# Maxima passes of a causal attention stage as one stream over its blocks, block 1's in the stage before, and both borders of the stage woven

## The reference

```python
# C: attention
q = x @ Wq + bq; k = x @ Wk + bk; v = x @ Wv + bv
scores = jnp.einsum('bqd,bkd->bqk', q, k) / jnp.sqrt(jnp.float32(hd))
scores = jnp.where(causal, scores, -jnp.inf)
weights = jax.nn.softmax(scores, axis=-1)
out = jnp.einsum('bqk,bkd->bqd', weights, v) @ Wo + bo
# D: routed feed-forward
base_out = jnp.einsum('bsd,df->bsf', x, W_base) + b_base
shared_out = jnp.einsum('bsr,rf->bsf', jnp.einsum('bsd,dr->bsr', x, A_s), B_s)
gates = jax.nn.softmax(jnp.einsum('bsd,de->bse', x, W_router) + b_router, axis=-1)
topk_w, topk_i = jax.lax.top_k(gates, TOP_K)          # TOP_K = 2 of E = 6
...
routed_out = jnp.einsum('bser,erf->bsf', hw, B_r)     # hw: h times its expert's weight
return base_out + shared_out + routed_out
# around each layer: x = _layernorm(x + layer(x))
```

## Time and profile before

| what | us |
|---|---|
| median of 3 runs | 1553.93 (1552.56 to 1555.5) |
| the profiled execution's own time | 1553.85 |
| its span in the profile | 1552.1 |
| TensorE busy in the span | 1471.6 (95%) |
| VectorE busy | 1006.4 (65%) |
| ScalarE busy | 735.5 (47%) |
| GpSimd busy | 342.1 (22%) |
| mean granted clock of TensorE | 0.986 |

### The profile page before, as it was taken

One profiled execution on the slowest core, in us unless ns is written; L12 is line 12 of the kernel. 1 busy time (PEld: TensorE's weight loads), 2 busy tenths in 40 slices (PEclk: granted clock), 3 DMA queues, 4 the chain that ended last, 5 costly groups with the idle time before them and its releaser, 6 DMA issues.

```text
span 1552.1 us, 23859 instructions
## 1 busy us (share of the span) xinstructions
PE 1471.6 (95%) x9484; PEld 1008.5 (65%) x9484; DVE 1006.4 (65%) x1967; ACT 735.5 (47%) x1040; POOL 342.1 (22%) x259
## 2 busy tenths in 40 slices
PE   8999999999999977898999999989989998989998
PEld 6677777777777765444554555546656655567886
DVE  3355545464635455897778878775878877556665
ACT  4433333333333322878877876854334344442333
POOL 0021112121111122000000000001657676750001
PEclk9999999999999989999999999999999999999999
DMA  7203131303031150001101100014000000000112
GB/s 264 79 27 108 33 102 54 105 29 106 35 100 48 40 189 21 28 1 55 54 13 43 55 28 28 1 41 115 33 0 1 1 0 1 0 1 28 55 55 82
DMA packets 43904, 79.93 MB, mean 51 GB/s; under 512 B 7073, under 2 KB 14881, under 8 KB 42386
## 3 DMA queue, kind: packets, MB, share of 16 engines
q1 hardware_dynamic: 43794, 78.41, 15.0%
HBM read 53.24 MB, written 25.17 MB: 51 GB/s over the span
## 4 chain that ended last, share of the span: by engine, by line
PE 60%; issue 20%; DVE 14%; ACT 4%; POOL 2%; DMA 0%; SPq 0%; DVEq 0%; POOLq 0%; ACTq 0%
PE psum L125 12%; PE psum L127 11%; PE psum L126 11%; PE psum L1335 5%; PE psum L978 3%; PE psum L985 3%; DVE sm L447 3%; PE psum L594 2%; PE psum L620 2%; PE psum L1313 2%; PE psum L615 2%; PE psum L609 2%; DVE c_mx L1256 1%; PE psum L624 1%; PE psum L629 1%
## 5 line engine op out<-in xcount | busy, mean ns | idle before, releaser
L978 PE MATMUL psum<-early,high 128*128 128x512 fp8e4 x1024 | 234.5, 381 | 10.3 <-DVE low_r L950 4.2
L978 PEld LDWEIGHTS psum<-early,high 128*128 128x128 fp8e4 x1024 | 98.1, 98 | 132.1 <-ACT early L857 6.7
L1184 POOL TENSOR_TENSOR c_ls<-c_ls,c_pr 128x512 f32<-128x512 f32 (+2 forms) x136 | 161.6, 1188 | 66.1 <-ACT c_pr L1229 56.9
L393 POOL TENSOR_TENSOR rms<-ms,mhalf 128x16 f32<-128x16 f32 x32 | 93.1, 2911 | 364.4 <-DVE ms L456 364.4
L1229 ACT ACTIVATE c_pr<-c_sc 128x512 f32<-128x512 f32 (+2 forms) x144 | 85.4, 594 | 159.8 <-DVE c_sc L1271 145.4
L1335 PE MATMUL psum<-c_pr,V 128*128 128x512 f32 (+2 forms) x288 | 139.0, 568 | 5.2 <-ACT c_pr L1229 3.9
L125 PE MATMUL psum<-Qh,Kh 128*128 128x512 f32 (+1 forms) x272 | 141.9, 522 | 0.0
L1271 DVE TENSOR_TENSOR c_sc<-psum,c_mb 128x512 f32<-128x512 f32 (+2 forms) x144 | 92.1, 641 | 50.4 <-PE psum L127 37.4
L985 PE MATMUL psum<-high,b_act 128*128 128x512 fp8e4 x512 | 116.7, 382 | 0.3 <-ACT early L861 0.3
L125 PE MATMUL psum<-early_r,high_r 128*128 128x512 f32 x256 | 106.5, 416 | 5.4 <-DVE early_r L419 5.4
L127 PE MATMUL psum<-Qh,Kl 128*128 128x512 f32 (+1 forms) x272 | 104.8, 385 | 0.0
(11 more groups left out here) (230 smaller groups left out, 3248.8 us busy)
## 6 DMA issues: line engine op xcount, KB each, us to landing
low<-x_dram SPq DMA_DIRECT2D x9, 1024.0 KB, 5.6
wst<-in_L_ffn_w_gating SPq DMA_DIRECT2D x16, 512.0 KB, 4.5
xs<-in_L_attn_x SPq DMA_DIRECT2D x8, 1024.0 KB, 7.5
xt<-in_x_turned SPq DMA_DIRECT2D x7, 1024.0 KB, 4.9
x_dram<-xs SPq DMA_DIRECT2D x7, 1024.0 KB, 4.9
x_dram<-low SPq DMA_DIRECT2D x5, 1024.0 KB, 4.3
wst<-in_L_ffn_w_linear SPq DMA_DIRECT2D x16, 256.0 KB, 4.6
high<-x_dram SPq DMA_DIRECT2D x4, 1024.0 KB, 6.8
```

The costliest lines, as they stand in the source:

```text
L393: nc.gpsimd.tensor_tensor(rms[:, :], ms[:, :], const["mhalf"][:, 0:H], ALU.pow).then_inc(*done)
L978: last = t.matmul(out[:, h, :], w8g[:, tile + k, (2 * m + h) * P:(2 * m + h + 1) * P], x8[:, u, k, :], start=k == 0, stop=k == DC - 1)
L1184: nc.gpsimd.tensor_tensor(ls[:, i % 2, q0:], ls[:, i % 2, q0:], pr[:, g % SLOTS, q0:], ALU.add).then_inc(*L.done(*name))
```

## The change

**One stream.** The maxima of blocks 2 to 7, 132 jobs, are one list, taken along by all tiles of blocks 0 to 6 (112 tiles). Each block's maxima are due two tiles before its `mb`, and at each tile as many are taken as the tightest due time asks for, rounded up. This gives two at each of the first 22 tiles (blocks 0, 1 and ten tiles of block 2) and one at each tile after that. The number of maxima jobs in blocks 0 to 6 goes from 8, 12, 16, 20, 24, 28, 32 to 8, 16, 22, 16, 20, 24, 26.

**Block 1's maxima** leave block 0 for the end of stage B. The plan puts (1, 0, 0) and (1, 0, 1) after block 0's and the other six behind the bias row and the projections of block 7, two in a row at each place. A pair shares a bank (`w = 4 + name[2] % 2`), so its second matmul waits until VectorE has read the first. Block 0's own maxima move behind `y` (7, 0) and `y` (7, 1) of stage B.

**The weights of D**: ScalarE's high part is now made two tiles before VectorE's low part, which stays where it was.

**The opening of D**: `x` (0, 0) to (0, 3), `h` (0), `hN` (0), the gates of block 0 in six pieces and `hT` (0) are put between the last eighteen tiles of block 7. After the last `pv` come `x` (1), `rb` (0, 0), `L` (7), `rr` (0, 0), `h` (1), `y` (7, 0), `y` (7, 1), `hN` (1), `rb` and `rr` (0, 1), `y` (7, 2), `y` (7, 3) and the rest. The four `y` (7, c) use banks 7, 0, 1, 2 in place of 3, 7, 6, 7. The weighted result `hw` moves to a part of `Qh`, since `Ql` is still read then.

The core of the diff:

```diff
-    order = max_jobs(0) + [("mb", 0), ("bias", 0)]
+    order = max_jobs(0) + max_jobs(1)[:2] + [("mb", 0), ("bias", 0)] + max_jobs(1)[2:]
+    ahead = [job for i in range(2, NB) for job in max_jobs(i)]
+    due, n = [], -2
+    for i in range(1, NB - 1):
+        n += tiles(i)
+        due.append((n + tiles(0), sum(len(max_jobs(j)) for j in range(2, i + 2))))
...
-        ahead = max_jobs(i + 1) if i + 1 < NB else []
...
-            take = -(-len(ahead) // max(1, n - 2 - k)) if ahead else 0
+            gone = n_ahead - len(ahead)
+            take = max([-(-(jobs - gone) // (end - g)) for end, jobs in due if end > g and jobs > gone], default=0)
...
-        elif i == 0 and kind in ("mx", "mb"):
-            w = 4 + (name[2] % 2 if kind == "mx" else 0)
+        elif i == 0 and kind == "mb":
+            w = 4
+        elif i <= 1 and kind == "mx":
+            w = 4 + name[2] % 2
...
         elif kind == "y" and i == NB - 1:
-            w = (3, 7, 6, 7)[name[2]]
+            w = (7, 0, 1, 2)[name[2]]
...
-    order = [("x", 0, k) for k in range(DC)] + [("h", 0)] + [("x", 1, k) for k in range(DC)]
-    order += [("hN", 0), ("rb", 0, 0), ("rb", 0, 1), ("rb", 0, 2), ("hT", 0), ("h", 1), ("rr", 0, 0), ("hN", 1),
-              ("rr", 0, 1), ("rr", 0, 2), ("rb", 0, 3), ("rr", 0, 3), ("hT", 1)]
+    order = [("x", 0, k) for k in range(DC)] + [("h", 0), ("hN", 0)] + [("gate", 0, n) for n in range(6)] + [("hT", 0)]
+    order += [("x", 1, k) for k in range(DC)] + [("rb", 0, 0), ("rr", 0, 0), ("h", 1), ("hN", 1), ("rb", 0, 1), ("rr", 0, 1)]
+    order += [("rb", 0, 2), ("rr", 0, 2), ("hT", 1), ("rb", 0, 3), ("rr", 0, 3)]
...
+        plan += part("B", ("y", last, 3), ("VT", last - 1)) + part("C", ("mb", 0), ("mx", 1, 1, 1))
+        plan += part("B", ("VT", last - 1), ("V", last - 1)) + part("C", ("mx", 1, 1, 1), ("mx", 1, 2, 1))
+        plan += part("B", ("V", last - 1), ("Q", last)) + part("C", ("mx", 1, 2, 1), ("mx", 1, 3, 1))
+        plan += part("B", ("Q", last), ("VT", last)) + part("C", ("mx", 1, 3, 1), ("s", 0, 1)) + part("B", ("VT", last), None)
...
-        splits = {("s", 3, 2): 0, **{("s", 6, 3 * k + 2): k + 1 for k in range(DC + 1)}}
...
+        opening = {("pv", last, 14 + n): job for n, job in [(k, ("x", 0, k)) for k in range(DC)] + [(5, ("h", 0)), (7, ("hN", 0)), (15, ("hT", 0))]}
+        opening.update({("pv", last, 22 + n): ("gate", 0, n) for n in range(6)})
+        high_parts = {("s", 3, 0): 0, **{("s", 6, 3 * k): k + 1 for k in range(DC + 1)}}
+        low_parts = {("s", i, k + 2): n for (_, i, k), n in high_parts.items()}
```

More of the change, by code:

```diff
@@ L1078, in stage_c @@
         order += tail
+    assert not ahead
     order += [("L", NB - 1)] + [("y", NB - 1, c) for c in range(CH)]
@@ L1412, in stage_d @@
     gate = [(x, None) if isinstance(x, str) else x for x in gate]
-    dve_order, act_order, pool_order, counts = [], [], [], []
-    for n, name in enumerate(order):
+    gate_pieces = [gate[:3], gate[3:6], gate[6:10], gate[10:14], gate[14:19], gate[19:]]
+    pe_order, dve_order, act_order, pool_order, counts = [], [], [], [], []
+    for name in order:
         kind, b = name[0], name[1]
+        if kind != "gate":
+            pe_order.append(name)
         if kind == "x":
@@ L1424, in stage_d @@
         elif kind == "hN":
-            act_order.append(("exp", b))
-            dve_order += [(g, b, c) for g, c in gate]
+            if b:
+                act_order.append(("exp", b))
+                dve_order += [(g, b, c) for g, c in gate]
+        elif kind == "gate":
+            if name[2] == 0:
+                act_order.append(("exp", b))
+            dve_order += [(g, b, c) for g, c in gate_pieces[name[2]]]
         elif kind == "hT":
@@ new lines, in program @@
+        high_parts = {("s", 3, 0): 0, **{("s", 6, 3 * k): k + 1 for k in range(DC + 1)}}
+        low_parts = {("s", i, k + 2): n for (_, i, k), n in high_parts.items()}
+        for job in part("C", ("s", 0, 1), ("y", last - 1, CH - 1)) + part("C", ("y", last - 1, CH - 1), ("pv", last, NB * CH - 1)):
+            plan.append(job)
+            if job[1] in high_parts:
+                plan.append(("D", ("ahead", "act", high_parts[job[1]])))
+            if job[1] in low_parts:
+                plan.append(("D", ("ahead", "dve", low_parts[job[1]])))
+            if job[1] in opening:
+                plan.append(("D", opening[job[1]]))
```

38 lines of the change are left out of this document (21 added, 17 removed).

## The result

The changed kernel takes 1542.02 us (median of 4 runs, 1540.84 to 1543.87) against 1554.56 for the kernel before: ratio 0.9922, 95% interval 0.9905 to 0.9939. The profiled execution took 1540.84 with a span of 1539.1, 13.0 less than before, where the prediction had 23.8. The time lies outside the 1523 to 1537 that the prediction took as its own range, and inside its range for 8 cases in 10, 1519 to 1543.

The account below looks back on a forecast made before the run. TensorE, busy 95%, bounds the kernel, so time falls only where it waits, mostly for VectorE. Terms -2.0 - 21.5 + 5.9 - 6.2 = -23.8 take 1553.85 to 1530.1 us; own range 1523 to 1537, 8 in 10 within 1519 to 1543.

Parts of the forecast that it names:

- blocks 3 to 6: Attention blocks 3 to 6: fewer maxima and 6.6 of waits left, 170.9 in place of 192.3, -21.5 us.
- blocks 0 to 2: Attention blocks 0 to 2: ten more maxima, VectorE ends last, about 56 in place of 58.0, -2.0 us.
- border B/C: End of stage B: block 1's maxima and their pairs' waits for reductions cost +5.9 us, bounds +1.7 and +9.
- the rival I gave 0.15: Blocks 3 to 6: VectorE waits for GpSimd's bias addition, 1.75 per block, 7 more, 1537; chance 0.15.
- the backlog: Start of block 3: VectorE's backlog from block 2 adds 0.8 us of waiting.
- What waits stay?: Blocks 3 to 6: 1.2 per block at y tiles, 0.8 at block 3's start, 1.0 in block 6; together 6.6.
- in block 7 TensorE hardly felt it: Block 7: argument against GpSimd becoming the wait, as TensorE waited only 2.7 there in all.
- block 6's waits stay: Block 6: if ScalarE's casts delay c_pr, earlier casts only move the waits; 9 of 10.8 stay, 1539; chance 0.08.
- its queue is now never empty: Blocks 0 to 2: reason for taking about 56 us, with VectorE busy 55.3 and ending last.
- Border C/D: From the last pv to h (2), plus work moved into block 7: 37.9 against 44.12, -6.2 us, bounds -9 and -2.
- the wait of 3.3: Border C/D: x (1)'s low parts wait for ScalarE's hh behind four normalisations; 3.3 us allowed.
- The clock's rival: Blocks 1 and 2: brief TensorE stops halve its clock; 44 more over blocks 0 to 2, about 1574; chance 0.05.

Follow-up runs that it names:

- e10: Changed kernel with GpSimd's bias addition in four pieces, each y waiting for its own piece alone: 1534.20 us, ratio 0.9871.
- e9: Changed kernel without most of GpSimd's bias addition (64 columns of one chunk left, output incomplete): 1528.43 us, one run.
- e7: Kernel before with the one stream alone (blocks 1 to 7 in blocks 0 to 6): 1552.84 us against 1553.87, ratio 0.9998.
- e11: Kernel before with only ScalarE's casts of D's weights moved two tiles ahead of VectorE's: 1546.31 us, ratio 0.9942.
- e6: Changed kernel with the stream's maxima kept away from tiles with a y and spread evenly over the others: 1540.89 us, ratio 0.9916.
- e4: Changed kernel with y (7, 2) and y (7, 3) directly behind y (7, 1): 1543.26 us, ratio 0.9931.
- e2: Changed kernel with the stream of maxima at a truly even rate, 1.27 per tile: 1543.51 us, ratio 0.9939.
- e8: Changed kernel with y (7, 2) and y (7, 3) behind x (2) rather than behind rr (0, 1): 1537.26 us, ratio 0.9892.
- e12: Changed kernel with block 1's pairs in two banks, no maxima at y tiles, y (7, 2) and y (7, 3) behind x (2), bias in four pieces: 1533.94 us.
- e1: Changed kernel with border B/C as before, block 1's eight maxima back in block 0: 1537.73 us, ratio 0.9898.
- e3: Changed kernel with block 1's maxima in alternating banks in place of one bank per pair: 1534.57 us, ratio 0.9881.

## Why the prediction was off

The direction and the place of the gain held; the size did not, -13.0 in the span (-12.5 in the medians) against -23.8, and 1542 is above the prediction's own 1523 to 1537. Of the 10.8 that are missing, blocks 3 to 6 have 4.7, blocks 0 to 2 have 3.7, border B/C 1.9 and the half clock behind `h` (2) 1.35; the rest, -0.9, is ahead of the bias row and up to `h` (2).

- **Blocks 3 to 6: the rival I gave 0.15 came in.** The working, with waits of 1.2 per block, 0.8 for the backlog and 1.0 for casts, gave 170.9. With the bias in pieces these blocks take 169.3 (e10), so the count of work and of VectorE's waits was good. What failed is the step "What waits stay?", which left GpSimd's bias addition out of the sum: with it they take 175.5. As a rival I priced it at 1.75 per block, 7; e9 and e10 measure 6.8 and 6.2. That the price fits is partly luck: the rival had VectorE waiting for GpSimd at `y` in all four blocks, and in block 6 it was the low part that was held, for 2.6. Its evidence was also incomplete: rows 10 show block 7 alone, but the first `y` of blocks 4 and 5 already started 0.09 behind the addition's end in before. I held against it that "in block 7 TensorE hardly felt it". That looked at a block where VectorE had no maxima and could catch up; in blocks 3 to 6 a `y` tile costs it 0.31 more than TensorE as it is, and the wait comes on top.
- **The waits of block 3 and 6 were put down to the wrong part.** The prediction let them go because VectorE had fewer maxima, and gave the casts a remainder. e7 and e11 show that the stream alone leaves both (block 3 -0.2, block 6 -2.3), and that the casts' two tiles remove 3.9 and 6.1. The rival "block 6's waits stay" was wrong: moving ScalarE's part ahead did not just move the wait. Block 6 ended at 55.9 against 53.6.
- **Blocks 0 to 2: the step "its queue is now never empty" failed.** VectorE was busy 53.7, near the 55.3 reckoned, but in 60.2 rather than 56. In the four tiles with a `y` it is late (e6: -6.3 in blocks 1 and 2 with none there and 16 fewer in all), and around them it waits: 0.95 for `oh` in each of blocks 1 and 2, 1.0 for `mb`'s row in block 2, 0.5 and 0.3 for GpSimd's bias addition. A sum of busy times over three blocks is a lower bound, not the span.
- **Border B/C: the pairs as forecast** (5.0 of waits and 1.8 of work, less the 1.1 that TensorE waited for `Kl` in before as well); missing was the half clock behind the third one, 1.5, which e6 shows to be no part of the waits themselves: same instructions, same waits, clock 1.00, 17.18 in place of 18.74.
- **Border C/D: the wait of 3.3 and the -6.2 up to `h` (2) as forecast.** The half clock behind the wait cost 1.35 more; the sum had 1.5 for a low clock ahead of `h` (2), where the mean clock was 0.99, and nothing behind it.
- **The clock's rival did not come**: windows 1 and 2 have 1.00 with VectorE as their bound. By the Trainium skill, "TensorE: Matmul & The Clock Gate", section "A second HAM failure mode: psum-queue depth-cycling", brief idles between groups would make the clock swing; here five waits of up to 0.6, one of 1.0 and one of 1.6 in blocks 1 and 2 left it at full. Half clock followed single waits of 1.8 to 5.0 (third pair, `h` (2), block 3 before and in e7 and e11, e4's `hT`), and once one of 0.98 (e2). It did not follow the third pair's 1.93 in e6, the 3.27 at `h` (2) in e9, the 2.60 at `y` (7, 2) in e8 and e12, or the 1.80 at `mb` (3) in before, which e11 has too and which half clock followed there. What separates these can't be told from the runs.

What the parts are worth, from the table, adding up to after's -12.2: the casts -10.0 in blocks 3 and 6 (e11; -8.5 in all, with the half clock that moved); the stream -1.3 on top of them (e1 against e11, blocks 0 to 6: +5.4 in blocks 0 to 2, -6.7 in 3 to 6), and 0 without them (e7); block 1's maxima in stage B +4.0 as made (after against e1, up to `h` (2)), and -2.1 with two banks (e3 against e1); D's opening with the border -6.3, and +1.35 of half clock behind it. The last is a difference of columns; no run has it alone. So the one stream and block 1's maxima in stage B, with which the title begins, cost 2.7 together as made; the earlier high parts and D's opening brought the gain.

## What to carry to other kernels

When one engine is made lighter, ask which long single instruction it now reaches early: here VectorE arrived a microsecond and more sooner at a 4.6-us addition on GpSimd, and cutting that in four was worth 7 us. Look for such a wait by the times at which things end, since a list of waits names one engine of several. Put a cross-engine cast two steps ahead of its consumer before rebalancing anything, and give two matmuls in a row two banks. And in this kernel work that only has to be done by some time was better done early than evenly: the exact even rate and the placing away from `y` both lost in later blocks at least what they won in the first.
